# Two recurrent blocks on one core: layer 0's Q, K, V, router and expert up-products as one-pass products, experts by batch from streamed weight slots, a new order

## What is computed

```
xn = layernorm(x)
s  = attention(xn; 16 heads of 16, causal, softmax, with biases)        # layer 0
g  = silu(sum over the 2 best of 8 experts of  weight * (silu(xn w1) * (xn w2)) w3)
x  = x + s * g
xn = layernorm(x)
s  = gated delta rule(xn; 16 key heads of 128, 32 value heads, 4-tap convolutions, chunks of 128 rows)   # layer 1
g  = silu(2 shared experts + the 2 best of 16 routed experts)
x  = x + s * g
```

## Time and profile before

| | |
|---|---|
| median of the runs | 1414.15 us |
| the profiled execution, first to last instruction (span) | 1418.7 us |
| TensorE busy | 1338.4 us (94%), 12308 matmul records |
| VectorE / ScalarE / GpSimd busy | 1126.6 (79%) / 949.1 (67%) / 698.8 (49%) us |
| mean granted clock of TensorE | 0.978 of 2.4 GHz |
| layer 0, to the first product of layer 1 | 258.5 us |
| DMA | 76.68 MB |

### The profile page before, as it was taken

How to read it: one execution, slowest core, us unless ns; L and a number is a source line. 1 busy time by engine, 2 the same in 40 slices (tenths; PEclk the granted TensorE clock), 3 DMA queues, 4 the chain that set the end, 5 groups by cost and what they waited for, 6 DMA issues and landing times.

```text
span 1418.7 us, 32580 instructions
## 1 busy us (share of the span) xinstructions
PE 1338.4 (94%) x12308; PEld 1091.0 (77%) x12308; DVE 1126.6 (79%) x2294; ACT 949.1 (67%) x2607; POOL 698.8 (49%) x806
## 2 busy tenths in 40 slices
PE   6999999778999999999999999999999998999997
PEld 3544446667888879888889798888888987789896
DVE  4587436889979788969798879697888897988886
ACT  3105751476777768777778678677687777787774
POOL 8012222337754565464745655556555557555431
PEclk9979999889999999999999999999999999999999
DMA  9900001212101121131311311312212114111000
GB/s 320 191 5 1 4 1 45 75 40 72 44 25 37 31 87 35 31 88 33 85 37 32 91 31 39 83 30 76 46 32 68 43 31 116 38 31 31 24 2 31
DMA packets 59507, 76.68 MB, mean 54 GB/s; under 512 B 6200, under 2 KB 46776, under 8 KB 59352
## 3 DMA queue, kind: packets, MB, share of 16 engines
q1 hardware_dynamic: 54616, 60.31, 16.7%
q0 software_dynamic: 4736, 14.29, 3.6%
HBM read 62.92 MB, written 11.67 MB: 53 GB/s over the span
## 4 chain that ended last, share of the span: by engine, by line
PE 60%; DVE 20%; ACT 6%; issue 5%; DMA 4%; POOL 3%; another core or an unknown queue 1%; SPq 0%; POOLq 0%; DVEq 0%; ACTq 0%
PE ps L930 10%; PE ps L1313 6%; DVE yv L1644 4%; PE ps L977 4%; DMA RC<-crow 3%; PE ps L1218 3%; DVE yk L1644 3%; PE ps L1266 2%; PE ps L1295 2%; PE ps L1228 2%; PE ps L1231 2%; PE ps L985 2%; PE ps L1282 2%; PE ps L1267 2%; PE ps L1291 2%
## 5 line engine op out<-in xcount | busy, mean ns | idle before, releaser
L1988 ACT ACTIVATE XY<-ps 128x512 f16<-128x512 f32 x384 | 221.2, 598 | 88.6 <-PE ps L1231 75.2
L1734 DVE TENSOR_TENSOR ZL<-ps,cst 128x256 f16<-128x256 f32 x384 | 155.0, 418 | 47.4 <-PE ps L1218 40.8
L1644 DVE SCALAR_TENSOR_TENSOR yv<-ps,cw,yv 128x511 f32<-128x511 f32 (+2 forms) x192 | 143.3, 746 | 7.0 <-ACT yv L1925 2.3
L930 PE MATMUL ps<-XH,WVh 128*128 128x256 f32 (+1 forms) x384 | 133.9, 349 | 1.2 <-ACT hT L1973 1.2
L1313 PE MATMUL ps<-WO,OGT 128*128 128x256 f32 x512 | 126.8, 391 | 3.2 <-DVE OGT L1806 2.9
L930 PE MATMUL ps<-XH,WVl 128*128 128x256 f32 (+1 forms) x384 | 123.5, 322 | 0.0
L930 PE MATMUL ps<-XL,WVh 128*128 128x256 f32 (+1 forms) x384 | 123.3, 321 | 0.0
L2181 POOL TENSOR_TENSOR RC<-RC,dec 128x512 f32<-128x512 f32 x64 | 69.3, 1083 | 100.8 <-DMA RC<-crow 100.6
L1228 PE MATMUL ps<-ZL,XY 128*128 128x64 f16 x1536 | 105.7, 193 | 8.1 <-DVE ZL L1734 4.4
L1218 PE MATMUL ps<-XY,LT 128*128 128x64 f16 x1536 | 101.1, 193 | 12.9 <-ACT XY L1988 11.1
L1218 PEld LDWEIGHTS ps<-XY,LT 128*128 128x128 f16 x1536 | 80.0, 98 | 42.4 <-issue 20.1
(11 more groups left out here) (305 smaller groups left out, 4122.0 us busy)
## 6 DMA issues: line engine op xcount, KB each, us to landing
RC<-crow SPq DMA_DIRECT2D x128, 128.0 KB
WV<-in_WV SPq DMA_DIRECT2D x16, 512.0 KB, 3.6
WK<-in_WK SPq DMA_DIRECT2D x16, 256.0 KB, 2.7
WO<-in_WO SPq DMA_DIRECT2D x16, 256.0 KB, 2.8
rows_out<-st SPq DMA_DIRECT2D x7, 512.0 KB
KS<-spread SPq DMA_DIRECT2D x12, 256.0 KB, 12.1
QS<-spread SPq DMA_DIRECT2D x12, 256.0 KB, 16.5
w<-in_w SPq DMA_DIRECT2D x4, 512.0 KB, 8.7
```

The costliest lines, as they stand in the source:

```text
L930: m = pe.matmul(o, a, b, start=c + k == 0, stop=c == 1 and k == 2)
L1644: m = dve.scalar_tensor_tensor(out=dst[:, k:512], in0=ps[:, bk, 0:512 - k], scalar=cw[:, h, j, 3 - k:4 - k], in1=dst[:, k:512], op0=ALU.mu ...
L1734: leave(dve.tensor_tensor(half(ZL[:, k - 2], k, 0), p, lv(k), ALU.mult), "a", u, k)
L1988: leave(act.activation(changed(u, k), ps[:, bank("b", u, k), :].rearrange("p (c n t) -> p c n t", c=2, t=1 << (k - 1)), ACT.Copy), "b", u, k)
```

## The change

- **Products.** Q, K and V, the router and the experts' up-products use `three` on XH and XL, which now also hold layer 0's turned rows: ScalarE writes XH (L1828), VectorE the rest XL, eight new instructions. xnT is gone. GpSimd splits wqk, wv and each expert's w1 and w2. V and the router are one product of 264 columns (256 of V and 8 logits); V is stored in 17 columns a head, the last of them one. Its eviction is two VectorE instructions. The operation `rt` is gone.
- **Experts.** Order by batch, k = 8b + e. Weights of an expert are one array of 768 columns in one of three slots. The first three are loaded at the start; each further one is operation `fx`: SP waits for the down-products of k - 3 and issues 384 KB, GpSimd splits 512 of the columns; the up-products wait for the split.
- **Stacks.** `qk` runs batch by batch, `spread` is written by batch, and `stack` is issued in SP's searched list, batch 1 apart from batch 0. The products for the maxima read 48 rows, the scores 50; two DMAs write the two rows of ones of KS from MT, and GpSimd's large fills of KS and QS are gone. Small loads (bo, wo, wab, rows, nwc, cw, WK of heads 0 and 1) follow stack 1.
- **Batches.** `ln1` of a batch waits for that batch's up-products only. `ready(b)` adds the last down-products.
- **Order.** RANK is new, `rt` dropped, and a second table LATER adds up to 4.07 us to a part's start time in the key that picks it; all of ORDER1 is computed anew, layer 1 included.

```diff
@@ Plan.arrange
-                key = int(at / self.GRAIN), p.rank
+                key = int((at + p.later) * (1 / self.GRAIN)), p.rank
@@ plan_experts0
-    P.add(("rt",), -160, ("PE", 3.6), ("DVE", 0.3), takes=True, gives=("rt",))
...
-        e, b = divmod(k, 2)
+        b, e = divmod(k, 8)
...
+        if k > 2:
+            P.add(("fx", k), rank, ("SP", 3.0, *old), ("POOL", 1.75))
+        else:
+            P.add(("fx", k), rank, ("POOL", 1.75))
+        P.add(x, rank, ("PE", 1.32, (("fx", k), "POOL")), ("ACT", 0.62, *old), takes=True, gives=x)
@@ plan_rows0
+        experts = [((w, e, b), "PE") for w in ("exg", "exv") for e in range(8)]
@@ ready
-    return [(("ln1", 4 * b + 3), "DVE"), (("pv", 1, 3, 3), "PE")]
+    return [(("ln1", 4 * b + 3), "DVE"), (("pv", 1, 3, 3), "PE"), (("exd", 7, 1, 0), "PE"), (("exd", 7, 1, 1), "PE")]
@@ run_sync
+            for k in range(3):
+                fetch_expert(k)
+            w.wait_ge(s_ones, 3)
+            for r in range(2):
+                sp.dma_start(KS[64 * r + 48:64 * r + 50]..., MT[0:2, :]... .broadcast_to((2, 8, 1024))).then_inc(d_ones, 16)
             for b in range(2):
+                at = slice(512 * b, 512 * b + 512)
+                for t in (2, 3, 0, 1):
+                    w.wait_ge(*done("qk", t, b))
+                    for k, part in enumerate((CH, CL)):
+                        sp.dma_start(spread[k, 128 * t:128 * t + 128, at], part[:, t, at].bitcast(F32)).then_inc(
+                            d_spread[t // 2, k, b], 16)
...
+                if what == "stack":
+                    stack(h)
+                    if h == 1:
+                        fetch_small()
+                elif what == "fx":
+                    for q in range(2):
+                        w.wait_ge(*full("exd", (h - 3) % 8, (h - 3) // 8, q))
+                    fetch_expert(h)
@@ run_tensor
+            w.wait_ge(s_wqs, 1)
+            for b in range(2):
...
+                        m = three(ps[:, bk, :], wqkh[:, c, 128 * t:128 * t + 128], wqkl[:, c, 128 * t:128 * t + 128],
+                                  XH[:, c, at], XL[:, c, at], c)
...
+                    m = three(ps[:, bk, 0:264], XH[:, c, at], XL[:, c, at], wvh[:, c, :], wvl[:, c, :], c)
...
+                    w.wait_ge(s_exs, k + 1)
                     for c in range(2):
-                        m = pe.matmul(ps[:, bk, :], wt[:, c, e, :], xnT[:, c, 512 * b:512 * b + 512],
-                                      start=c == 0, stop=c == 1)
+                        k0 = 128 * c + (256 if what == "exv" else 0)
+                        m = three(ps[:, bk, :], exh[:, k % 3, k0:k0 + 128], exl[:, k % 3, k0:k0 + 128],
+                                  XH[:, c, at], XL[:, c, at], c)
@@ run_vector
+            for n in range(NT):
+                at = slice(128 * n, 128 * n + 128)
+                w.wait_ge(s_xh0, n + 1)
+                leave(dve.tensor_tensor(XL[:, :, at], ps[:, bank("ln0", n), 0:256]...,
+                                        XH[:, :, at].bitcast(F32), ALU.subtract), "ln0", n)
@@ run_gpsimd
-            for p0 in (32, 96):
-                pool.memset(KS[p0:p0 + 32].bitcast(F32), 1.0).then_inc(s_ones, 1)
-                pool.memset(QS[p0:p0 + 32].bitcast(F32), 0.0).then_inc(s_ones, 1)
...
+            w.wait_ge(d_qk, 32)
+            split(wqk, wqkh, wqkl, s_wqh, s_wqs, 1)
+            w.wait_ge(d_v, 32)
+            split(wv[:], wvh[:], wvl[:], s_wvh0, s_wvs, 1)
...
+                if x[0] == "fx":
+                    split_expert(x[1])
```

More of the change, by code:

```diff
@@ L64 @@
 RANK = {
[4 rows of a table removed]
[L69 to L80, removed]
@@ new lines @@
+    "p1": {"DVE": 154.5, "PE": -3.57}, "pl": {"POOL": -83.22}, "pre": {"ACT": -80.34, "DVE": 83.16},
[3 rows of a table added]
+    "so": {"DVE": 132.76, "PE": -125.29}, "spg": {"POOL": -18.02}, "sq": {"ACT": -3.34, "POOL": -61.39},
+    "sr": {"DMA": 96.01, "POOL": 10.86}, "ss": {"SP": 59.93}, "stack": {"SP": -78.23},
+    "su": {"ACT": 128.73, "PE": -5.34}, "sw": {"DMA": 26.52, "POOL": 22.63}, "tn": {"DVE": -142.73, "PE": -0.69},
+    "tn0": {"DVE": 38.74}, "top": {"ACT": -61.77, "DVE": -22.01}, "tp": {"ACT": -1.36, "DVE": 123.3},
@@ L103, in __init__ @@
         self.label, self.eng, self.cost, self.after, self.rank, self.takes = label, eng, cost, after, rank, takes
+        self.later = LATER.get(label[0], {}).get(eng, 0.0)
         self.gives, self.left, self.due = None, len(after), 0.0
@@ L197, in plan_softmax0 @@
 def plan_softmax0(P):
-    P.add(("stack", 0), -300, ("SP", 20.0))
-    P.add(("stack", 1), -300, ("SP", 26.0, (("stack", 0), "SP")))
+    P.add(("stack", 0), -300, ("SP", 14.0))
+    P.add(("stack", 1), -100, ("SP", 16.0, (("stack", 0), "SP")))
     for b in range(2):
@@ L238, in plan_rows0 @@
         P.add(("xr", b), -9, ("SP", 3.0, (("nr2", b), "DVE")))
-    experts = [((w, *divmod(k, 2)), "PE") for w in ("exg", "exv") for k in range(16)]
     for n in range(NT):
         b = n // 4
+        experts = [((w, e, b), "PE") for w in ("exg", "exv") for e in range(8)]
         old = [(("ln1", n - 1), e) for e in ("PE", "ACT", "DVE")] if n else [None] * 3
@@ L244, in plan_rows0 @@
               ("ACT", 0.4, old[1]), ("DVE", 0.42, old[2]), takes=True, gives=("ln1", n))
-    P.add(("spg",), -100, ("POOL", 1.0))
+    P.add(("spg",), -100, ("POOL", 1.0, (("stack", 1), "SP")))
     for h in range(2):
-        P.add(("fWK", h), -100, ("POOL", 1.9))
+        P.add(("fWK", h), -100, ("POOL", 1.9, (("stack", 1), "SP")))
     end = ("op", NT - 1), "DVE"
@@ L499, in place_products @@
         B.put(("ln0", n), every.next())
-    for t in (2, 3, 0, 1):
-        for b in range(2):
+    for b in range(2):
+        for t in (2, 3, 0, 1):
             B.put(("qk", t, b), every.next())
@@ L562, in room, with twins @@
             return [(s_free[b], n) for b, n in BANKS.prior[key]]
-        def twins(first, second, shape):
+        def twins(first, second, shape, scope=None):
             here = ExitStack()
@@ L598, in build @@
         wabh = sb("wabh", [128, 2, 80], F32R)
-        wqk = WK[:].rearrange("p a c n -> p (a c n)").rearrange("p (c n) -> p c n", c=2)
+        wqk, wqkh, wqkl = (a[:].rearrange("p a c n -> p (a c n)").rearrange("p (c n) -> p c n", c=2)
+                           for a in (WK, WKh, WKl))
         sc = ExitStack()
@@ L1495, in run_vector @@
                 what = x[0]
-                if what == "rt":
-                    take_logits(x, lg0, 8)
-                elif x == ("tp", 1):
+                if x == ("tp", 1):
+                    for n in range(NT):
+                        w.wait_ge(*done("v0", n))
                     best_two(0, lg0, 0)
```

226 lines of the change are left out of this document (115 added, 111 removed), and 18 rows, old and new, of the table RANK.

## The result

The changed kernel takes 1450.93 us (median of 4, 1448.67 to 1459.15), the kernel before 1415.47 beside it: ratio **1.0249, 95% interval 1.0219 to 1.0278**. The forecast was 1374 us and 0.97 for faster. It was wrong in size and in sign; this part looks for the 77 us between the two.

The account below looks back on a forecast made before the run. TensorE's work was taken to bound the kernel, except in four stretches of layer 0 and behind it, some set by VectorE. The terms summed to -40.0 us from the median of 1414.15: 1374 us, range 1356 to 1391.

Parts of the forecast that it names:

- Order of layer 1: New ranks and LATER reorder all queues of layer 1; nothing in the trace prices it; taken as 0, bounds +8 and -8 us.
- The gap between the layers: From last down-product to layer 1's first product: VectorE work moved under batch 1's work; -10 us, between -3 and -17.
- rival (a): Between the layers: batch 1's gates and decays set the first inverse, only 3 of 10 us come; 1381 or 1385; chance 0.16.
- TensorE's work as time: In layer 0 shorter products shorten the run: Q and K -2.7, V and router -11.4, expert up-products -12 us.
- Q and K: Head of layer 0: cheaper products, -2.7 us; later start behind the low halves XL, +0.8 us (0 to 3).
- The stage of the maxima: Row maxima of layer 0: half of some 8.5 us lost to VectorE's pace and low clock returns, -4.3 us (0 to -8.5).
- the clock behind the router: Behind the router in layer 0: without its narrow products the full clock is expected, -1.7 us (0 to -1.7).
- Streamed weights: 13 expert weight refills in layer 0, hidden on a free queue but not behind the stacks; one stop taken, +3 us.
- (b): A refill lands behind a stack; TensorE goes through batch 0's maxima alone at low clock; 1379 to 1391; chance 0.10.
- (d): Slower: every refill is late, at the wait for the split in front of exg; 1423 at 4 us each; chance 0.02.
- (e): A one-pass product is as slow as a full one; called excluded by layer 1's rows; "same as before" got 0.01.
- The last down-product near 211: Sign that the change works as forecast: layer 0's last down-product near 211 us, layer 1's first product within 2 us of it.

Follow-up runs that it names:

- e1: Changed kernel with every engine taking layer 1's parts in the sequence of the kernel before; ratio to the kernel before 0.9958, 1410.7 us.
- e2: Changed kernel with the sequence of the kernel before only for layer 1's start-up, the rest in the new order; ratio to the kernel before 1.0004.
- e12: Changed kernel with one RANK number, tn on PE, moved from -0.69 to -0.70, which turns an exact tie; ratio to the kernel before 0.9877.
- e9: e8 with one of the three products of each layer 0 expert up-product left out, 64 matmuls less; ratio to the kernel before 0.9866.
- e10: Kernel before with the gate half of expert up-products summed over 128 of 256 rows, 16 of 64 matmuls less, order kept; ratio 0.9937.
- e7: e1 with GpSimd splitting the Q/K weights only after VectorE's 8 scalings; ratio to the kernel before 0.9964.
- e8: e1 with both the edit of e6 and the edit of e7; ratio to the kernel before 0.9893.
- e6: e1 with SP's loads of batch 0's stack issued ahead of the spreads of batch 1; ratio to the kernel before 0.9901.
- e13: e12 with the two edits of e8; ratio to the kernel before 0.9810, 1370.6 us on a chip where the kernel before takes 1398.2.
- e3: Changed kernel with batch 1's chain of first gates, row sums, norms, transposes, gt and gg taken 20 us of plan earlier; ratio to the kernel before 1.0260.
- e14: Changed kernel with layer 1's start-up taking keys, values, gates and routing at the places of the kernel before; ratio to the kernel before 1.0178.

## Why the prediction was wrong, step by step

**The step that failed is "Order of layer 1 ... I take 0", with bounds of 8 us.** The new order of layer 1 cost 41 us (e1), 35 of them in its start-up (e2), and with one tie broken the other way 53 us came back (e12). "Nothing in the trace prices a new order" was true of the trace, but the plan functions of both kernels held a price, an end 35.5 us later by their own costs, and I did not work it out. I drew the bounds from the steady part, a third of the 2.6% in which TensorE stands still there. They bound what can be won there, not what can be lost in the start-up, where the kernel before already had 11.28 us of idle TensorE in a hundred; with a worse sequence the changed kernel has 29.15. Idle time that is there says nothing about idle time that an order can add.

*The gap between the layers, -10.* The gap closed, and rival (a), that the chain through the gates of both batches sets the first inverse, fits what came of it. With the old sequence (e1) layer 1's first product is 9.1 us earlier than before and the first inverse 3.3. The rival's prices, 1381 and 1385, kept everything else of the sum; they are as far off as the forecast.

*TensorE's work as time.* The terms for Q/K, V, router and up-products were counted one to one, since the timeline showed "the engine without a gap". V with router was sized to the tenth: 38.26 - 32.35 = 5.9 us, 11.3 saved. An up-product between other work takes 191.62 - 190.12 = 1.50 us against 1.48 forecast, but 32 of them take 51.5 us from start to start and not 47, after 59.9 before: 8.4 saved and not 12. Of 170 of these records that are followed by another of them, 14 come at the pitch of the lower clock, which is some 3 of the 4.5 us. Q and K take 13.8 us from first to last product where they took 13.95. And e9 and e10 show that 0.4 to 0.5 of a saving in the up-products reaches the layer's end. So the 26 us of these terms were 20, and an estimate by one half of it is 10; for V and router no run took the work out alone.

*Q and K, -2.7 +0.8.* V starts 4 us later instead of 2 earlier: the products of Q and K start at 18.56, not 14.51, and end at 32.35, not 28.46. Two causes. The scalings took 6.82 us beside GpSimd's split, where I had written that the split "costs nothing". And the first 12 records come every 0.43 us, from 24.2 on every 0.23. Here I had weighed a rule of the Trainium skill, "SBUF — State Buffer", "Who interferes with whom", and put it aside by a row of GpSimd. e7 now bears the rule out from VectorE's side: 2559 ns beside a GpSimd subtraction, 485 at most with GpSimd made to wait. The row that would have told me stands in the trace of before, four of the same scalings (L1325) without and with GpSimd at work:

```profile
252.22 1.66 DVE L1325 SCALAR_TENSOR_TENSOR st<-xt,small 128x256 f32<-128x256 f32 x4
...
260.70 2.88 DVE L1325 SCALAR_TENSOR_TENSOR st<-xt,small 128x256 f32<-128x256 f32 x4 [2.53 <-POOL small L2111]
```

It was the rule that spoke against the change, and I priced it on GpSimd alone. At the head of layer 0 it costs next to nothing in the end (e7, e8); what the 13 splits behind refills cost VectorE later on, no run separates.

*The stage of the maxima, -4.3, and the clock behind the router, -1.7.* The dip behind the router is gone; in its place TensorE waits 3.40 us for the stack and works at half clock behind that (windows):

```profile
50.00:60.00 10.00, 6.60 (x28) 3.49 (x26) 5.35 (x12) 0.00 (x0) 3.69 (x4) 0.74 0.65 163
60.00:70.00 10.00, 10.00 (x47) 4.89 (x46) 8.90 (x12) 0.00 (x0) 1.88 (x2) 0.50 1.08 184
```

I had let the stack come early as "it no longer waits for a queue filled with w1, w2, w3"; that is so, but SP issued it behind batch 1's spreads. Issued in time it is worth 8 us with the old order of layer 1 (e6).

*Streamed weights, +3, rivals (b) and (d).* No wait of TensorE for a split or a refill stands in layer 0 of the changed kernel: 0, not 3. Rival (d) was named as the one on the slower side, and it is not what happened. (e) is excluded by the rows above.

*The last down-product near 211.* It starts at 241.55, and in e12 the last sixteen records start at 228.02, in e13 at 218.13. All eight output projections and the transposes of batch 0 now stand ahead of it, where before three projections stood behind; the term of -1.7, one more projection moved behind it, went the other way. Where they fall is again the order's doing.

*What is left.* With the old sequence of layer 1 the change is worth 6 us (e1), not 40. Of the 34 between, 16 are the halving and mis-sizing of TensorE's terms (26 counted, 10 by the estimate above) and 8 the late stack (e6); the other 10, about as much as the whole term of the gap, are not separated by a run.

What stays open: why this sequence starves the inverse. One chain moved (e3) and the places of keys, values, gates and routing taken back (e14) did not bring the time back, so it is none of these by itself; which parts block each other was not found.

## What to carry to other kernels

A list planner's order is part of the change: when operations or costs change, first compare the planner's own end before and after, for here it gave 35.5 us of loss, about what was measured, before anything ran. Then look for exact ties and plan the kernel again from several near tables, and time the orders before judging the operations: a hundredth in one rank was worth 53 us, and the new operations under the better order gain 17. Bound a new order by what the start-up can lose, not by the idle time of the steady part. And an engine that shows no gap is not proof that its work is the time: take a known amount of work out and see how much of it arrives.

## What the runs showed of the hardware

- A VectorE scaling with both inputs in SBUF and a GpSimd subtraction did not run side by side: one scaling of 0.48 us took 2.56 beside a subtraction of 2.40 us, and with GpSimd waiting none took over 0.485 (e7). Beside a GpSimd fill of 6.92 us the same scalings kept their 0.48 us (kernel before), and VectorE's subtractions for XL, with one input in PSUM, took 0.42 us beside GpSimd's cast and subtraction (e7), where their mean in the kernel before is 0.41.
- The Q/K products from 18.56 to 24 us come every 0.43 us and later ones of the same shape every 0.23, while the granted clock of that stretch is shown as 1.00. A 512-column product has that pitch of 0.43 from 285.00 us on too, and there the granted clock of 285 to 288 us is shown as 0.50, the level of 1.2 GHz. Ahead of the Q/K products TensorE had only 16 transposes, in three bursts with waits of 1.73 and 0.75 us between and 0.67 behind them. In e7, with no stop among the transposes but 2.63 us behind them, the first eleven come at 0.43 too, and the stage is 13.6 us long (17.18 to 30.75). The pitch of a known shape says more here than the clock column.
- A wait of 3.4 us for a transfer, up to 54.70 us, was followed by a granted clock of 0.50 from 60 to 70 us (above). With a wait of 4.98 us the clock of 50 to 80 us was 0.56 (e1), without a wait 0.83 (e6).
